# A selective-scan block whose scan output is summed token-major in PSUM, by accumulating transposes

## The reference, cut to what matters

```python
x = x + 0.5 * ffn(layernorm(x))          # 8 experts, the best one for each token
x = x + scan_layer(layernorm(x))
x = x + 0.5 * ffn(layernorm(x))

def scan_layer(x):                       # D_INNER 256, D_STATE 16, D_CONV 4
    xc, z = split(x @ W_in)
    xc = silu(causal_conv(xc) + conv_b)
    dt_r, Bm, Cm = split(xc @ W_x)
    dt = softplus(dt_r @ W_dt + b_dt);  A = -exp(A_log)
    # for each token t, channel d, state s:
    h = exp(dt_t * A) * h + (dt_t * x_t) * B_t
    y_t = sum over s of h * C_t
    y = (y + xc * D_skip) * silu(z)
    return layernorm(y @ W_out) * ln_g + ln_b
```

## Time and profile before

| what | value |
|---|---|
| median of 3 runs | 478.31 us |
| lowest and highest run | 478.08 and 481.46 us |
| span of the profiled execution, first to last instruction | 477.1 us |
| busy over the span | PE 417.0, DVE 331.4, ACT 284.8, POOL 272.4 us |
| the 64 scans | 143.7 us, the first at 167.4, the last at 344.8 |
| the 256 instructions of the adds | 121.1 us |
| the 512 transposes of the injects | 69.7 us |

### The profile page before, as it was taken

One profiled execution on the slowest core, in us unless ns is written; L12 is line 12 of the kernel. 1 busy time (PEld: TensorE's weight loads), 2 busy tenths in 40 slices (PEclk: granted clock), 3 DMA queues, 4 the chain that ended last, 5 costly groups with the idle time before them and its releaser, 6 DMA issues. The chain is left out here.

```text
span 477.1 us, 7572 instructions
## 1 busy us (share of the span) xinstructions
PE 417.0 (87%) x2544; PEld 321.3 (67%) x2544; DVE 331.4 (69%) x490; ACT 284.8 (60%) x546; POOL 272.4 (57%) x190
## 2 busy tenths in 40 slices
PE   7929988994988898979998999999993978998994
PEld 6829988994433754545655666566673968998894
DVE  3825445543997689957997998888878782553552
ACT  3204333421879699979999999999614404342340
POOL 3053656541018197968797999999902025666543
PEclk9778999997999899979999999999997797999799
DMA  7991211203002102221222332332135042111100
GB/s 223 304 267 33 46 41 35 46 23 106 0 3 84 58 33 100 88 90 45 88 90 88 117 104 90 116 105 89 44 150 203 2 100 43 36 43 47 33 27 29
DMA packets 25160, 38.99 MB, mean 82 GB/s; under 512 B 4450, under 2 KB 17315, under 8 KB 25123
## 3 DMA queue, kind: packets, MB, share of 16 engines
q1 hardware_dynamic: 22178, 32.38, 21.0%
q0 software_dynamic: 2944, 6.13, 5.3%
HBM read 33.19 MB, written 5.31 MB: 81 GB/s over the span
## 5 line engine op out<-in xcount | busy, mean ns | idle before, releaser
L789 POOL TENSOR_TENSOR w_sb<-phase,w_sb 128x1024 f32<-128x1024 f32 x63 | 152.8, 2449 | 22.2 <-DVE phase L869 21.7
L869 DVE TENSOR_TENSOR_SCAN phase<-phase,psum 128x1024 f32<-128x1024 f32 x64 | 143.7, 2275 | 22.2 <-PE psum L977 19.6
L992 PE MATMUL psum<-w_sb,ident 128*128 128x512 f32 x256 | 121.1, 598 | 0.4 <-POOL w_sb L789 0.4
L921 ACT ACTIVATE phase<-dtxT,B_cols 128x256 f32<-128x256 f32 x256 | 105.4, 494 | 6.1 <-PE psum L977 5.5
L634 PE MATMUL psum<-phase 128*128 128x128 f32 x736 | 95.5, 286 | 0.1
L634 PEld LDWEIGHTS psum<-phase 128*128 128x128 f32 x736 | 91.9, 203 | 0.2 <-issue 0.2
L977 PEld LDWEIGHTS psum<-ident,phase 128*128 128x128 f32 x512 | 60.7, 143 | 44.3 <-issue 16.8
L364 POOL DMA_INDIRECT phase<-token_rows,token_row x46 | 46.2, 1005 | 55.8 <-DMA token_rows<-x_tok 21.6
L977 PE MATMUL psum<-ident,phase 128*128 128x128 f32 x512 | 69.7, 279 | 9.6 <-ACT B_cols L829 3.4
L931 ACT ACTIVATE phase<-dt,neg_A 128x1024 f32<-128x1024 f32 x64 | 70.0, 1136 | 0.0
L992 PEld LDWEIGHTS psum<-w_sb,ident 128*128 128x128 f32 x256 | 44.4, 193 | 33.2 <-issue 32.6
(11 more groups left out here) (172 smaller groups left out, 347.0 us busy)
## 6 DMA issues: line engine op xcount, KB each, us to landing
w_sb<-c_rows SPq DMA_DIRECT2D x32, 512.0 KB, 3.6
w_sb<-ffn_w SPq DMA_DIRECT2D x16, 512.0 KB, 7.3
token_rows<-x_tok SPq DMA_DIRECT2D x8, 264.0 KB, 4.7
w_sb<-ffn_w SPq DMA_DIRECT2D x8, 256.0 KB
x_tok<-attn_x SPq DMA_DIRECT2D x4, 256.0 KB, 4.3
x_tok<-x_rows SPq DMA_DIRECT2D x4, 256.0 KB, 3.9
phase<-token_rows,token_row POOLq DMA_INDIRECT x46
x_rows<-phase,token_row POOLq DMA_INDIRECT x23
```

The costliest lines, as they stand in the source:

```text
L789: nc.gpsimd.tensor_tensor(hC[:, k % HC_RING, :], H[:, k % H_RING, :], C_sb[:, j % C_RING, :], ALU.mult).then_inc(M["hC_ready"], 1)
L869: nc.vector.tensor_tensor_scan(H[:, k % H_RING, :], dA[:, k % DECAY_RING, :], dBx_bank[k % SLOTS], 0.0, ALU.mult, ALU.add).then_inc(M["sca ...
L921: nc.scalar.activation(scaled[:, (j % SCALED_RING) * TB + t, :], dtxT[:, tile, :], ACT.Copy, scale=B_cols[:, tile, s:s + 1]).then_inc(M["s ...
L992: mm = nc.tensor.matmul(psum[:, Y_AT + 2 * h + q, :], ident[:], hC[:, k % HC_RING, q * CH:(q + 1) * CH], start=b > 0 and s == 0, stop=s == ...
```

## The change

- y is summed token-major. For every unit, `add` issues eight transposes of 128x128, C*h as the stationary operand and the identity moving, which accumulate in PSUM (`is_transpose=True`, `start` only on the first one into a bank). A bank holds two token tiles with both halves; `y_bank` is now by chunk.
- The skip term of both batches goes by PE: `skip(b, t)`, two matmuls of 128 columns for a token tile, behind the adds of units 8, 10, ... 22 of each batch. The DVE step is gone, and so are the four matmuls at the head.
- z is made token-major: `gates(c)`, the tokens as the stationary operand, 256 columns of W_in moving, four matmuls a chunk.
- The gate is by chunk, token-major, and waits for all adds of its batch. The add of unit 32 waits for both gates of batch 0; that of unit 33 for none.
- The gated y is turned back for the projection: `turn_yz(g)`, eight transposes a chunk, and `hold_yzT(g)`, a copy by ACT into the place of xc. The first two use the banks of injects with even k, the others those of y.

The diff, without the lists of semaphores and with the unchanged lines left out:

```diff
-        y_bank = [two_banks(Y_AT + 2 * h) for h in range(NH)]
+        y_bank = [two_banks(Y_AT + 2 * q) for q in range(CPB)]
+        yzT = xc
+        yzT_bank = [dBx_bank[0], dBx_bank[0], y_bank[0], y_bank[1]]
+        SKIP_BEHIND = range(8, 8 + 2 * TB, 2)
...
             def gate(g):
-                b, h = divmod(g, NH)
-                dve.wait_ge(M["summed"], KB * (b + 1) - NH + h + 1)
-                if b:
-                    nc.vector.scalar_tensor_tensor(out=y_bank[h], in0=xc[:, h, batch[b]], scalar=D_skip_sb[:, h:h + 1],
-                                                   in1=y_bank[h], op0=ALU.mult, op1=ALU.add
-                                                   ).then_inc(M["skip_added"], 1)
-                    dve.wait_ge(M["skip_added"], h + 1)
-                nc.vector.tensor_tensor(silu_z[:, h, batch[b]], y_bank[h], silu_z[:, h, batch[b]], ALU.mult
-                                        ).then_inc(M["yz_ready"], 1)
+                b, q = divmod(g, CPB)
+                dve.wait_ge(M["summed"], KB * (b + 1))
+                rows = silu_z[:, g * GROUP:(g + 1) * GROUP, :].rearrange("p j m -> p (j m)")
+                nc.vector.tensor_tensor(rows, y_bank[q], rows, ALU.mult).then_inc(M["yz_ready"], 1)
...
+            def hold_yzT(g):
+                act.wait_ge(M["yzT_psum"], g + 1)
+                nc.scalar.copy(yzT[:, :, chunk[g]].rearrange("p h (j t) -> p j h t", t=P),
+                               yzT_bank[g].rearrange("p (j h t) -> p j h t", j=GROUP, h=NH)
+                               ).then_inc(M["yzT_ready"], 1)
...
             for b in range(B):
+                for q in range(CPB):
+                    hold_yzT(b * CPB + q)
                 rows_out(b)
...
+            def y_at(t, h):
+                return psum[:, Y_AT + t // 2, (t % 2) * NH * P + h * P:(t % 2) * NH * P + (h + 1) * P]
+
             def add(k):
                 b, s, h = UNITS[k]
-                if b and not s:
-                    pe.wait_ge(M["yz_ready"], (b - 1) * NH + h + 1)
+                if b and not s and not h:
+                    pe.wait_ge(M["yz_ready"], b * CPB)
...
-                for q in range(CPB):
-                    mm = nc.tensor.matmul(psum[:, Y_AT + 2 * h + q, :], ident[:],
-                                          hC[:, k % HC_RING, q * CH:(q + 1) * CH], start=b > 0 and s == 0,
-                                          stop=s == S - 1)
+                for t in range(TB):
+                    mm = nc.tensor.matmul(y_at(t, h), hC[:, k % HC_RING, t * P:(t + 1) * P], ident[:], is_transpose=True,
+                                          start=not s and not h and t % 2 == 0, stop=k % KB == KB - 1 and t % 2 == 1)
                 mm.then_inc(M["summed"], 1)
 
-            def skip(b, h):
-                for q in range(CPB):
-                    nc.tensor.matmul(psum[:, Y_AT + 2 * h + q, :], D_diag[:, h, :],
-                                     xc[:, h, b * L + q * CH:b * L + (q + 1) * CH], start=True, stop=False)
+            def skip(b, t):
+                for h in range(NH):
+                    nc.tensor.matmul(y_at(t, h), xc[:, h, b * L + t * P:b * L + (t + 1) * P], D_diag[:, h, :],
+                                     start=False, stop=False)
+
+            def turn_yz(g):
+                pe.wait_ge(M["yz_ready"], g + 1)
+                if g < CPB:
+                    pe.wait_ge(M["scan_done"], K - SLOTS + 1)
+                if g % CPB:
+                    pe.wait_ge(M["yzT_ready"], g)
+                for j in range(GROUP):
+                    for h in range(NH):
+                        at = (j * NH + h) * P
+                        last = nc.tensor.transpose(yzT_bank[g][:, at:at + P], silu_z[:, g * GROUP + j, h * P:(h + 1) * P],
+                                                   ident[:])
+                last.then_inc(M["yzT_psum"], 1)
 
             def project(b):
-                pe.wait_ge(M["yz_ready"], NH * (b + 1))
-                pe.wait_ge(M["scan_done"], K - SLOTS + b + 1)
+                pe.wait_ge(M["yzT_ready"], CPB * (b + 1))
+                if not b:
+                    pe.wait_ge(M["scan_done"], K)
...
-            skip(0, 0)
             for k in range(K):
...
-                if k == 0:
+                if k == 1:
                     pe.wait_ge(M["relu_dve"], 1)
-                    skip(0, 1)
                 if k >= 1:
                     add(k - 1)
+                    if (k - 1) % KB in SKIP_BEHIND:
+                        skip((k - 1) // KB, SKIP_BEHIND.index((k - 1) % KB))
...
+            turn_yz(0)
             add(K - 1)
-            for b in range(B):
-                project(b)
+            turn_yz(1)
+            project(0)
+            turn_yz(2)
+            turn_yz(3)
+            project(1)
...
+                def gates(c):
+                    pe.wait_ge(M["norm"]["xnT_ready"], max(c, 1 + 2 * (c % 2)) + 1)
+                    if c >= 2:
+                        pe.wait_ge(M["silu_z_ready"], c - 1)
+                    for j in range(GROUP):
+                        tile = c * GROUP + j
+                        mm = nc.tensor.matmul(psum[:, NG + 2 * (c % 2) + j // 2, j % 2 * DI:(j % 2 + 1) * DI],
+                                              xnT[:, tile * P:(tile + 1) * P], W_in_sb[:, DI:2 * DI],
+                                              start=True, stop=True)
+                    mm.then_inc(M["z_psum"], 1)
```

More of the change, by code:

```diff
@@ L889, in recurrence_vector @@
                 if b and at in (1, 2):
-                    gate((b - 1) * NH + at - 1)
+                    gate((b - 1) * CPB + at - 1)
             dve.wait_ge(M["scan_done"], K)
@@ L895, in recurrence_vector @@
                                     C_sb[:, (len(PAIRS) - 1) % C_RING, :], ALU.mult).then_inc(M["hC_last"], 1)
-            for h in range(NH):
-                gate((B - 1) * NH + h)
+            for q in range(CPB):
+                gate((B - 1) * CPB + q)
             norm_vector(dve, M["out_norm"], y_row, arrives=[(M["o_ready"], g + 1) for g in range(NG)])
@@ L938, in rows_out @@
                     act.wait_ge(M["o_psum"], (c + 1) * GROUP)
-                    nc.scalar.copy(y_tok[:, c * GROUP * D:(c + 1) * GROUP * D], psum[:, 2 * b + q, :]
+                    nc.scalar.copy(y_tok[:, c * GROUP * D:(c + 1) * GROUP * D], psum[:, 2 * (1 - b) + q, :]
                                    ).then_inc(M["o_ready"], 1)
@@ L1009, in project @@
                     for h in range(NH):
-                        mm = nc.tensor.matmul(dBx_bank[b][:, j * D:(j + 1) * D], silu_z[:, h, rows], W_out_sb[:, h, :],
+                        mm = nc.tensor.matmul(dBx_bank[1 - b][:, j * D:(j + 1) * D], yzT[:, h, rows], W_out_sb[:, h, :],
                                               start=(h == 0), stop=(h == NH - 1))
@@ L1257, in turn_xn, with inner @@
                     last.then_inc(M["norm"]["xnT_psum"], 1)
-                def inner(c, z):
-                    pe.wait_ge(M["norm"]["xnT_ready"], max(c, 1 + 2 * (c % 2) if z else c) + 1)
+                def inner(c):
+                    pe.wait_ge(M["norm"]["xnT_ready"], c + 1)
                     if c >= 2:
-                        pe.wait_ge(M["silu_z_ready"] if z else M["xc_pre_ready"], (c - 1) * (1 if z else NH))
+                        pe.wait_ge(M["xc_pre_ready"], (c - 1) * NH)
                     for h in range(NH):
-                        m = z * NH + h
-                        mm = nc.tensor.matmul(psum[:, z * NG + 2 * (c % 2) + h, :], W_in_sb[:, m * P:(m + 1) * P],
-                                              xnT[:, chunk[c]], start=True, stop=True)
-                        if not z:
-                            mm.then_inc(M["xc_psum"], 1)
-                    if z:
-                        mm.then_inc(M["z_psum"], 1)
+                        nc.tensor.matmul(psum[:, 2 * (c % 2) + h, :], W_in_sb[:, h * P:(h + 1) * P],
+                                         xnT[:, chunk[c]], start=True, stop=True).then_inc(M["xc_psum"], 1)
+                def gates(c):
[8 more added lines that the diff above has]
+                    mm.then_inc(M["z_psum"], 1)
                 turn_xn(0)
                 turn_xn(1)
-                inner(0, 0)
-                inner(1, 0)
-                inner(0, 1)
+                inner(0)
+                inner(1)
+                gates(0)
                 turn_xn(2)
                 turn_xn(3)
-                inner(2, 0)
-                inner(1, 1)
-                inner(3, 0)
-                inner(2, 1)
-                inner(3, 1)
+                inner(2)
+                gates(1)
+                inner(3)
+                gates(2)
+                gates(3)
                 def project(c):
```

9 lines of the change are left out of this document (5 added, 4 removed).

## The result

The changed kernel took 487.06 us (median of 4 runs, 486.24 to 490.96), the kernel before beside it 479.75 (4 runs, 478.08 to 481.46): a ratio of 1.022, 95% interval 1.017 to 1.027. The forecast was 483.4, in the range 479.5 to 487.5 and slower, but at a ratio of 1.011. The direction and what bounds the kernel came out; the price of the idle times did not. As a ratio the loss is twice the forecast one; in time it is 7.3 us between the medians and 8.3 between the profiled executions, for 5.1.

A forecast was written before the change was run, and what follows sets the result against it. ACT, at 2.64 us a unit against PE's 2.59, was taken as the bound; -0.7 us to the last scan, +5.3 tail and +0.5 clock there made +5.1, 482.2 profiled and 483.4 as median, range 479.5 to 487.5.

The forecast's parts named there:

- What bounds: Recurrence: ACT needs 2.64 us a unit against PE's 2.59, so quicker PE work below 2.64 buys nothing more.
- The new add: PE, each unit: eight accumulating transposes cost 0.87 us like an inject, instead of 1.72, bounds 0.87 and 1.8.
- C: Rival: an accumulating transpose is priced as a matmul, PE stays at 2.59 us a unit; +8.3, 486.6 us, chance 0.10.
- D: Rival: transposes do not hold the clock, a unit takes 3.5 us on PE; about 544 us, chance 0.04.
- The lag: End of the recurrence: the last scan follows ACT's end more closely, at 344.7 instead of 347.10; -2.4 us.
- The wait of 0.74: ACT's wait for inject 17, late because of PE's adds, disappears; -0.74 us.
- DVE's waits for decays: Recurrence, a predicted sign: DVE waits for ACT's decays instead of for PE.
- Skip and in-projection: Skip matmuls move into free PE time, 0; in-projection keeps the same columns and ACT elements, 0, bounds +-0.3 us.
- The tail's order: After the last scan: turns, copies and projections step by step, 17.7 us instead of 12.4; +5.3 us.
- the price of the clock: PE's clock may fall after idle times: +0.8 at unit 18, +0.4 at unit 28, +0.5 us in the tail.
- The gate: Batch 0, add of unit 32: PE idles 3.6 us, delaying ACT's scales of units 40 and 41; +1.2, bounds 0 and +2.7.
- A: Rival: not slower, the clock stays up at units 18, 28, the gate and the tail; 480.5 us, chance 0.25.

The follow-up runs named there:

- e5: Changed kernel plus 20, 12 and 5 zero-matrix products keeping PE busy before it waits at units 14, 18 and 28; ratio 1.013 to the kernel before.
- e0: The changed kernel again, unchanged, run as a partner beside the later experiments; ratio 1.015 to the kernel before.
- e1: Kernel before, with one of the two long matmuls left out of each add except for the first and last state; ratio 1.007 to the kernel before.
- e4: Changed kernel with all four tail turns ahead of both projections, each in its own pair of PSUM banks; ratio 1.011 to the kernel before.
- e8: The kernel of e7 with two scales in eight on DVE instead of one; ratio 1.135 to the kernel before.
- e10: Same kernel as e7, run on one chip beside the kernel before with one scale in eight on DVE; ratio 0.993 to the kernel before.
- e7: Changed kernel with zeros on PE, four turns first in own banks, batch 0's gates together, one scale in eight on DVE; ratio 0.990 to the kernel before.

## Why the prediction fell short

**Right.** What bounds: ACT's 2.64 a unit stayed (5.28 a pair), PE had slack, and the steady stretch gained nothing. The new add: 0.87 us for eight, the inject's price, with the clock at 1.00; that refutes C, and D too. By the rule of the Trainium skill (TensorE: Matmul & The Clock Gate, Part 4), D should have come; the trace speaks against it: from 305 to 315 us, 63 of PE's 71 instructions are transposes (the other 8 are the skip's), at granted clock 1.00. The lag: 347.42 - (341.71 + 2.20) = 3.5 us against 5.9, the forecast -2.4. The wait of 0.74 is gone. DVE's waits for decays came as well. Skip and in-projection: no wait in the after trace points at either; they were not run alone. The tail's order came step for step: 17.7 forecast, 19.75 - 1.53 (5.37 - 3.84, the clock in the last projection) = 18.2 measured, some 0.5 dearer, spread over its hand-offs; e5, with the clock up there, has the same 18.2.

**The failed step is the price of the clock.** I had bounds of 0 and +1.7 at each unit and of 0 and +3 in the tail, and took parts of them: +0.8 at unit 18, +0.4 at unit 28, +0.5 in the tail. All three fell, and the units' were paid whole: 2.71 - 1.01 = +1.7, 2.64 - 1.07 = +1.6, and +1.5 in the tail. That is 4.8 us for 1.7. The bounds were right and the weights in them too low. The whole price is no rule either: the same kernel in e0 paid 0.4, +1.6 and +1.5, because at unit 18 the clock fell during the injects. Which of the two it will be, no run here lets one forecast: sixteen injects took 3.67 us after 3.29 of idle time, 2.41 after 2.69, and 2.40 after 3.60 in e1. What could be had from the rows is this. At 18 the idle time that I worked out (2.8) and the one measured (3.29) were nearer to 3.43, which fell, than to 2.05, which stayed. At 28 I counted the idle before the injects (1.43 measured) and overlooked the one just ahead of the turn: 1.97 us, then sixteen instructions (turn and add), then 1.43. A fifth place, the inject at 189.45, was missed altogether, and cost nothing only because hardly anybody waited for it.

**The gate was over-sized.** PE waited 3.33 us there as worked out (3.6) and the clock fell, but ACT lost 0.23 and not 1.2. Two things set that number. One is how late ACT is by then: in the changed kernel it is 2.2 us later (-0.74, -0.3 at unit 14, +1.7, +1.6). It asks for its injects 11.92 us after scan 33 has started, in e5 after 11.27, and PE needs 4.34 us from that add to inject 37 in both; ACT's waits are 0.23 and 0.89. The other is when the clock falls: in e4 ACT is as late, but the add behind the gate runs low from its start (1.97 us for eight instead of 1.42), and ACT waits 0.87. So the terms are not independent, and I summed them as if they were.

**The sum, mended:** -2.4 - 0.74 - 0.3 + 1.7 + 1.6 + 0.2 = +0.1 up to the last scan (+0.2 measured), +5.8 + 1.5 in the tail, +0.7 outside: 8.1 of 8.3. The 0.7 was in no term and stays open; outside stage and tail e0 and e5 differ by 1.8 us, with next to no edit there. The profiled executions differ by 8.3, the medians by 7.3, so about 1 us of this is scatter from run to run.

**The rivals.** A (clock up everywhere) would have been 480.5, 2.2 us above the kernel before. e5 comes nearest to it: stage and tail together are 2.0 us above the kernel before's, but its clock fell at the gate, and the 1.7 us that it gained at unit 14 are not in A. Of A's condition, both idle times that I put below 2.05 lost their clock anyway. The measured 487.06 lies nearest to C's 486.6, and inside my range because C is in it: that is luck, since the adds took C's price nowhere. (C's own terms, 3.6 and 5.3, add up to 8.9 and not to 8.3.)

## What to carry to other kernels

When two engines lie 2% apart, work taken off the lighter one buys nothing in the steady stretch, and every idle time that it makes can cost TensorE its clock at the next burst: look for what waits for that burst before counting the gain. Price a state that may flip by its cases, say which one the forecast takes, and keep the others as rivals with their full price; filler that holds the clock up helps only while the engine behind it is still late. And when several such places follow each other on one chain, let each one start from the delay that the last has left. A second layout turn at the end of a stage is priced by its hand-offs (turn, copy, turn in the same bank), not by its instructions: separate banks, with all turns ahead of both projections, gave back 5.2 of 7.4 us, the clock's 1.5 among them.

## What the runs showed of the hardware

- A fp32 transpose that accumulates into PSUM costs the same as one that doesn't: 0.87 us for eight of 128x128.
- The length of the last idle time alone does not tell whether the clock falls: it stayed after 2.05 us, and fell after 1.97 us at unit 28 in the changed kernel (in e5 it stayed after the same 1.97, with zeros behind the turn). With the same idle times in the tail it fell in the changed kernel and in e0, and stayed in e5. This is the granted clock of the changed kernel in its last projection, after idle times of 1.19 and 1.10 us around a turn of eight (columns as above):

```profile
361.00:364.00 3.00, 2.82 (x13) 2.82 (x14) 0.00 (x0) 0.13 (x1) 0.00 (x0) 0.50 0.55 218
364.00:365.00 1.00, 1.00 (x9) 1.00 (x9) 0.00 (x0) 0.20 (x1) 0.00 (x0) 0.80 0.04 12
```

- A 128x256 scale on DVE from SBUF to SBUF took 0.32 us with POOL idle at its start, and lasted until 0.15 us behind the end of POOL's running product when 0.3 us or more of that was left: 2.47 us in e8, 0.56 in e10, where it regularly met the last 0.4 us of a product. One scale in e8 and one in e10 outlasted two products, 4.7 us. The Trainium skill, SBUF — State Buffer, "SBUF: two separate sides", says that VectorE and GpSimd share one pair of SBUF ports, that a GpSimd instruction or a VectorE one in a 2-port mode or with two SBUF inputs holds it under an exclusive lock for the whole instruction, and that the other blocks. The trace agrees with the blocking in e8, e7 and e10, and does not show which mode a scale ran in; no run moved a scale against a product on purpose. The scans, which read one operand from PSUM, kept their 2.27 us beside the same products.
